# Cross-attention turns: the flip of the weighted rows moves behind the weighting, the last prob chunk behind the projection

## What is computed

```python
q = einsum('bsd,df->bsf', layernorm(x), Wq) + bq        # 32 samples, 64 rows of 256
k = einsum('bsd,df->bsf', ctx, Wk) + bk                 # ctx: 32 x 1601 x 256
v = einsum('bsd,df->bsf', ctx, Wv) + bv
probs = softmax(q @ k.T)
x1 = probs @ v + layernorm(x)
x  = x + layernorm(x1) * gamma + beta
```

## Time and profile before

| | before |
|---|---|
| timed runs, us | 543.02, 544.65, 545.02 (median 544.65) |
| profiled execution, span | 541.7 |
| TensorE matmuls | 497.2 busy (92%), x5012 |
| TensorE weight loads | 347.4 (64%) |
| VectorE | 399.4 (74%) |
| ScalarE / GpSimd | 200.2 (37%) / 198.7 (37%) |
| chain that ended last | TensorE 70%, DMA 9%, VectorE 6%; L1109 15%, L1133 15% |

### The profile page before, as it was taken

The page is one execution under the profiler, slowest core; times in us unless marked ns, Lnnn a source line. Parts: engine busy times, 40 slices in busy tenths (PEclk is TensorE's granted clock), DMA queues, the critical chain, the costliest instruction groups (busy, mean ns, idle before and its releaser), DMA issues.

```text
span 541.7 us, 14453 instructions
## 1 busy us (share of the span) xinstructions
PE 497.2 (92%) x5012; PEld 347.4 (64%) x5013; DVE 399.4 (74%) x1068; ACT 200.2 (37%) x617; POOL 198.7 (37%) x314
## 2 busy tenths in 40 slices
PE   7998999999999999999999998999979979999960
PEld 7665666656666666666656566666735568888840
DVE  3699799999899999999562678788775325555545
ACT  2343422432332233333311566655431035555500
POOL 4000413112222221122222666665776615665620
PEclk9999999999999999999999999999998989999995
DMA  7999679786988988884017999310122235554249
GB/s 278 349 354 273 204 237 321 269 215 201 304 279 291 300 291 287 282 274 139 21 44 212 278 299 310 117 51 2 50 88 80 96 109 158 162 146 123 76 163 302
DMA packets 67348, 108.83 MB, mean 201 GB/s; under 512 B 8115, under 2 KB 49125, under 8 KB 67304
## 3 DMA queue, kind: packets, MB, share of 16 engines
q1 hardware_dynamic: 60888, 97.83, 58.0%
q0 software_dynamic: 3792, 8.43, 4.5%
q10 hardware_dynamic: 2624, 1.97, 1.2%
HBM read 85.31 MB, written 24.85 MB: 203 GB/s over the span
## 4 chain that ended last, share of the span: by engine, by line
PE 70%; DMA 9%; DVE 6%; POOL 5%; issue 4%; ACT 4%; SPq 1%; ACTq 0%; POOLq 0%; DVEq 0%
PE banks L1109 15%; PE banks L1133 15%; PE banks L1515 8%; DMA ring<-in_ctx_dram 4%; POOL rows_by_expert L727 4%; PE banks L1527 4%; PE banks L1121 3%; DVE ctxT L1637 3%; PE banks L1146 3%; PE banks L1068 2%; PE banks L1509 2%; PE banks L1249 2%; PE banks L1242 2%; PE banks L1265 2%; DMA xn_all<-expert_out 2%
## 5 line engine op out<-in xcount | busy, mean ns | idle before, releaser
L1637 DVE STREAM_TRANSPOSE ctxT<-ring 128x832 f32<-128x832 f32 x128 | 121.7, 1007 | 4.7 <-DMA ring<-in_ctx_dram 4.7
L1109 PE MATMUL banks<-ctxT,qT_all 32*64 32x416 f32 (+2 forms) x2048 | 93.9, 498 | 1.9 <-issue 1.2
L1133 PE MATMUL banks<-ring,prob 128*64 128x256 f32 (+1 forms) x832 | 93.6, 381 | 0.7 <-ACT prob L839 0.7
L1133 PEld LDWEIGHTS banks<-ring,prob 128*64 128x64 f32 (+1 forms) x832 | 58.6, 137 | 31.5 <-issue 4.2
L1109 PEld LDWEIGHTS banks<-ctxT,qT_all 32*64 32x64 f32 x2048 | 56.9, 131 | 30.6 <-issue 13.4
L638 POOL TENSOR_TENSOR var<-mv,eps 128x1 f32<-128x1 f32 x32 | 6.3, 196 | 166.8 <-DVE mv L1682 114.8
L761 POOL DMA_INDIRECT expert_out<-prob,dest x47 | 46.2, 984 | 40.5 <-DVE prob L2098 26.6
L852 ACT ACTIVATE prob<-banks,negmax 128x416 f32<-128x416 f32 (+2 forms) x80 | 41.1, 531 | 30.2 <-DVE negmax L1659 30.2
L1515 PE MATMUL banks<-ring,ctxT 128*128 x188 | 50.2, 391 | 0.0
L674 POOL TENSOR_TENSOR ctxT<-ctxT,k_mask 128x1088 f32<-128x1088 f32 x16 | 33.1, 2069 | 30.8 <-ACT ctxT L930 30.8
L839 ACT COPY prob<-banks 128x512 f32<-128x512 f32 x64 | 27.5, 514 | 38.1 <-PE banks L1121 38.1
(11 more groups left out here) (269 smaller groups left out, 939.4 us busy)
## 6 DMA issues: line engine op xcount, KB each, us to landing
ring<-in_ctx_dram SPq DMA_DIRECT2D x48, 1024.0 KB
qT_all<-q_by_pair SPq DMA_DIRECT2D x56, 128.0 KB, 9.0
rows_by_expert<-blank SPq DMA_DIRECT2D x8, 774.0 KB, 6.8
ctxT<-rows_by_expert SPq DMA_DIRECT2D x47, 129.0 KB, 2.1
mid<-stage SPq DMA_DIRECT2D x31, 128.0 KB, 2.3
ring<-in_ctx_dram SPq DMA_DIRECT2D x16, 130.0 KB
ctxT<-mid SPq DMA_DIRECT2D x16, 128.0 KB, 3.9
qT_all<-mid SPq DMA_DIRECT2D x16, 128.0 KB, 4.6
```

The costliest lines, as they stand in the source:

```text
L1109: last = pe.matmul(S[a][64 * b:64 * b + 64, 0:KW[a]], q_rep[mine, r, c, 64 * b:64 * b + 64], ctxT[mine, c, b, 0:KW[a]], start=c == 0, stop ...
L1133: last = pe.matmul(U[64 * b:64 * b + 64, 0:D], probT[0:rows, k, 64 * b:64 * b + 64], ring[0:rows, r, b, k, :], start=k == 0, stop=k == KT)
L1637: dve.transpose(ctxT[:, c].rearrange("p b (k j) -> p (b k) j", j=Q), ring[:, r].rearrange("p b k c -> p (b k) c")[:, :, columns(c):columns ...
```

## The change

On TensorE the flip of pair i-2 stands behind the weighting of pair i-1; the first three prob chunks follow it; then comes the projection, then the last chunk. On ScalarE the exponents stand ahead of the copy of `UT`. On VectorE `normalise(k)` gets one more wait, for UT_done, since `Un` is now read later than before. The tail behind turn 15 isn't changed.

```diff
@@ ScalarE, turn
+                if ahead:
+                    exps(i)
                 if back2:
                     UT_evac(i - 2)
-                if ahead:
-                    exps(i)
@@ TensorE
-            def turn_probs(i, first=False):
+            def turn_probs(i, first=False, parts=KPARTS):
 
                 pe.wait_ge(exp_done, (i + 1) * len(EXPS))
                 for g, ks in enumerate(KPARTS):
+                    if ks not in parts:
+                        continue
                     if g == len(KPARTS) - 1 and not first:
                         pe.wait_ge(Un_ready, i)
@@ TensorE, turn
+                if back1:
+                    pe.wait_ge(Un_ready, i - 1)
+                    weigh(i - 1, (r - 1) % RING)
                 if back2:
                     if back3:
                         pe.wait_ge(res_ready, i - 2)
                     flip(i - 2)
-                if back1:
-                    pe.wait_ge(Un_ready, i - 1)
-                    weigh(i - 1, (r - 1) % RING)
-                if back2:
-                    project(i - 2)
                 if rows:
                     pe.wait_ge(xnT_copied, 2 * rows + 4)
                 if queries:
                     pe.wait_ge(qT_copied, 2 * queries + 2)
                 if ahead:
-                    turn_probs(i)
+                    turn_probs(i, parts=KPARTS[:-1])
+                if back2:
+                    project(i - 2)
+                if ahead:
+                    turn_probs(i, parts=KPARTS[-1:])
@@ VectorE
-            def normalise(k):
+            def normalise(k, first=False):
 
                 dve.wait_ge(pv_done, (k + 1) * len(KPARTS))
                 dve.wait_ge(rinv_ready, k + 1)
+                if not first:
+                    dve.wait_ge(UT_done, k)
                 dve.tensor_scalar(Un[:, :], U[:, 0:D], rinv[:, 0:1], None, ALU.mult).then_inc(Un_ready, 1)
@@
-            normalise(0)
+            normalise(0, first=True)
```

## The result

The change makes the kernel slower: 548.6 us (median of four runs, 548.23 to 554.57) beside 544.01 (four runs). The ratio is 1.0111, its 95% interval 1.0063 to 1.016. 546.2 was forecast, with a range up to 548.2. The profiled execution took 548.35, its span is 545.9 where before's was 541.7.

A forecast was written before the change was run, and what follows sets the result against it. TensorE's own order and the way through VectorE's Un were both taken to bind plain turns. Terms -0.2 + 0.90 + 0.84 = +1.5 us put the span at 543.2, the time at 546.2, range 542.6 to 548.2.

The forecast's parts named there:

- part 1: TensorE's order: flip behind weighting, project behind three prob chunks; its own order gets 0.19 us shorter per plain turn.
- part 4: ScalarE, exponents before the copy of UT: slack shrinks to 0.47 us, copy hidden by prob chunks; no cost.
- Un + 0.80: End of a turn: the next scores can't start before 0.80 us after VectorE's normalise (Un) starts.
- -0.1 over ten plain turns: Plain turns: the new TensorE order gains 0.1 us in all, with bounds of 0 and 1.9.
- Part 2: Plain turns: the last chunk still waits for Un, so they gain 0.1 us; with staged turns the sum is -0.2.
- Rival B: TensorE alone decides: ten plain turns save 0.19 us each and the tail 0.3, giving 542.4; chance 0.12.
- Part 3: VectorE's new UT_done wait in normalise is met 1.6 us early: cost 0, bounds 0 and 0.15 per turn.
- Rival C: The new wait delays VectorE's normalise by 0.15 us in turns 2 to 15, giving 548.3; chance 0.14.
- -0.05: Turn 5: TensorE's new order saves 0.05 us, where the flip already stood behind 128x128 work.
- Part 5: VectorE's residual waits for the later project: 0.90 us lost at turns 3 to 4, 0.84 in the tail.
- Rival D: The residual's delay is absorbed by ring blocks or store coming sooner; nothing is left, 544.6 us; chance 0.20.
- Part 6: SyncE: loop ring loads aren't moved relative to the scores, so nothing comes of it; turn 7's stall stays.

The follow-up runs named there:

- e12: Kernel before the change plus a long-met wait for const_step at the head of TensorE's turn_probs; 544.13 us, 1.0001 to before.
- e8: Kernel before the change plus a second, already met wait for exp_done ahead of the last prob chunk; 549.83 us, 1.0086 to before.
- e11: Same kernel as e8 (old order plus repeated exp_done wait), run again on another chip; 545.04 us, 1.0022 to before.
- e1: Changed kernel with exp_done waited for once per turn instead of twice; 547.1 us, 1.0064 to before.
- e5: Kernel of e4 with turns 2 to 5 back in TensorE's old order; 544.82 us, 1.0004 to before.
- e6: Kernel of e5 with the last prob chunk moved to scores bank 1, turned first, not waiting for Un; 543.04 us, 0.9964 to before.
- e7: Kernel before the change with only the last prob chunk freed from Un, as in e6; 544.07 us, 0.9982 to before.
- e10: Kernel before the change plus only VectorE's new UT_done wait in normalise; 544.34 us, 1.0007 to before.
- e3: Changed kernel with ScalarE's four query stores ahead of the copy of UT in turns 3 and 5; 548.96 us, 1.0078 to before.
- e2: Changed kernel with turn 15 alone in TensorE's old order; 546.93 us, 1.0048 to before.
- e9: Changed kernel run once more, unchanged, on another chip; 548.87 us, 1.0096 to before.
- e4: Changed kernel with the edits of e1, e2 and e3 together; 544.86 us, 1.0008 to before.

## Why the prediction was wrong, point by point

Two steps failed, each a term that the sum had at nothing: the wait for the exponents that the split repeats (part 1; 1.0 us in the turns and some 0.8 outside them), and the query stores behind the copy of UT (part 4; 0.5 us). The two losses that were forecast came.

- **Part 1, TensorE's order: right in each start, but a wait was overlooked.** The plan took over "Un + 0.80" for a chunk whose instructions had changed. The diff repeats `wait_ge(exp_done)` for the second call of `turn_probs`. I priced the moved matmuls and not this line, although a wait that is met looks free (and is where it brings no instruction, e12). Measured: 0.91 for 0.80, +0.11 in each plain turn, in the change, in e8 and in e11; gone in e1. The term "-0.1 over ten plain turns" is +0.76 over the seven undisturbed ones, and about +1 over the nine of the loop (there are nine, not ten). Its load of code at the end comes on top, some 0.8. The Trainium skill ("Perfetto Trace Analysis", Identifying Dependency Chains) notes that an instruction which waits on several engines may have separate semaphore instructions put ahead of it. The trace agrees: TensorE has 232 semaphore instructions for 218, and the load's idle time is put down to issue instead of Un. The Trainium skill has no price there; 0.11 us is this case's.
- **Part 2, Un binds: right.** e5 shows that the 0.19 is worth nothing beside Un, e6 that it is worth 0.19 without Un, e7 that removing Un alone is worth nothing in such a turn. Rival B, which wanted TensorE alone to decide, falls with it, and its mechanism comes true only in e6. The rule of the Trainium skill that part 2 cites ("Perfetto Trace Analysis", Identifying the Most-Contended Engine) judges TensorE by its weight loads and would name VectorE as the only bound. In e7 TensorE's loads are busy in 9.58 of 14.36 and its matmuls in all of it, and the turn doesn't get shorter. In e6 it does, to 14.17, by TensorE's order alone: VectorE has the same work (13.55 for 13.46). The measurement decides against the rule here.
- **Part 3, the wait for UT_done: right** at 0 (e10). Rival C forecast the sign and nearly the size, 548.3, by a mechanism that e10 shows to cost nothing. That it lay nearest is no support for it.
- **Part 4, ScalarE: wrong by omission.** The exponents and the copy of UT were followed, the query stores behind the copy weren't. They are moved behind a flip that comes late, 0.5 us of queue each, and prob copies stand behind them. Measured: 0.55 of wait at the scores of turn 4, and +0.53 in turn 5 (0.42 of it the stores), where "-0.05" stood. In turn 4 it costs nothing beyond the late residual (e3).
- **Part 5, the late residual: right in place and size.** Turn 3: 1.26 later for 1.27, and +1.00 for +0.90; e5 takes it back. Tail: +0.75 for +0.84; the store's landing took over the 0.29 of slack as worked out, and e2 takes it back. Turn 2, with bounds of 0 to 0.38, can't be told. Rival D (absorbed) falls.
- **Part 6, SyncE: no contradiction.** In the first profile the late ring load cost turn 8 (15.33) more than turn 7 (15.08); in e9 it is turn 7 again (15.80, and 14.88). Its place and size vary between runs of one kernel, so its 0.39 is not counted against the change.
- **The base.** 544.65 was the median of three runs; four have 544.01. The 3 us added to the span mix two things: the time around the span, 1.75, and the distance between executions. The forecast for the change itself was +1.5, measured +4.6.

The sum by steps: 1.0 (turns 3, 4) + 0.75 (tail) were forecast, 0.5 (turn 5) and 1.0 (the second wait) were missed. That gives 3.3. Each of the four is shown by undoing it and reading its turns. With the 0.8 outside the span it is 4.1, of 4.6 that the medians say (548.6 - 544.01). **What stays open:** the rest, 0.5 by the medians, 1.0 by those of e9 (5.2, of which 0.9 stand outside the span), and more by the ratio 1.0111, which would be 6. The intervals, from 1.0063 and 1.0062 up, start at 3.4 and take in 4.1. e4 took back 3.7, where its turns and the time outside the span give 2.9. The untouched end of the program differs by as much between kernels (260.6 to 263.7), and none of the runs separates this rest.

## What to carry to other kernels

When a block is split into two calls, count the waits that are issued twice: a met wait is free where it shares an instruction, but directly ahead of an instruction that waits for something else it can push that wait into an instruction of its own, here 0.11 us in every turn. The instruction count of the page tells it at once (14467 for 14453), and the instructions themselves can cost, here a further load of code at the program's end. When a step is moved on one queue, list what follows it on that queue up to the next instruction that somebody waits for, the DMA issues first. And where two engines end a loop turn at the same moment, shortening one gains nothing until the link between them is cut: here the link was one chunk's bank, and cutting it together with the shorter order made 0.36% where each alone made nothing that can be told.

## What the runs showed of the hardware

- **A late wait of TensorE costs differently by its form.** From Un to the second next operation 0.80 when the load itself waits, 0.91 when a semaphore instruction ahead of it does (before against e8, the change against e1).
- **Fourteen instructions more can cost at the end of the program.** They brought a 29th transfer of the instruction queue, 0.02 MB, and with it time above the span of 2.3 to 2.9 in 27 of 49 executions, never over 1.79 in 174 without.
- **The extra time of a turn with the loop's branch went with the wait ahead of it.** It was 0.36 to 0.4 in every third turn as long as the last chunk waited for Un, 0.07 at most in the one turn of e6 and of e7 that can be read.
- **DMA issues on ScalarE's queue hold its computing.** Four stores took 2.11 us in turn 3 and 1.83 in turn 5 (2.29 in e9), in which prob chunks that were ready stood.
- **Half clock came by chance here.** The granted clock was 0.66 in 281 to 286 of the change's profile, after 9 us in which TensorE was busy for 6.82, and the 16 turnings took 3.38 for 1.97. In e9 and e1, with the same late tail, they took 1.97. One profile of such a stretch is not enough to charge a change with it.
- **Fewer tile-size changes are worth what the rows said.** 14.36 to 14.17 from e7 to e6 is one change less a turn. The Trainium skill ("TensorEngine Tiling (Array Packing)", Key Properties) names a drain at such a change and no price; these rows agree that a change costs time, and give 0.19 us.
